# Two gated expert layers: the last two tiles of results placed by TensorE instead of scattered, results weighted by slot, rows numbered by partition

## The reference, cut to what matters

```python
probs = softmax(x @ router_w.T)
w, sel = top_k(probs, 2)
w = w / sum(w)
for g, u, d, c in experts:                     # c: this expert's weight for each token, 0 for most
    h = silu(x @ g) * (x @ u)
    acc = acc + c[:, None] * (h @ d)
x = x + tanh(g_ffn) * acc
```

## Time and profile before

| what | value |
|---|---|
| median of 3 runs | 814.03 us (810.46 to 814.49) |
| the profiled execution | 812.11 us, span of the trace 810.3 us |
| PE busy | 657.9 us, 81% of the span |
| POOL busy | 235.0 us, 29% |
| experts of layer 2, first gather to last result | 471.5 to 543.6 us |
| results of layer 2 kept to statistics done | 543.6 to 558.4 us |
| experts of layer 3, first gather to last scatter issued | 738.3 to 798.2 us |
| from there to the end | 798.2 to 810.3 us |

### The profile page before, as it was taken

One profiled execution on the slowest core, in us unless ns is written; L12 is line 12 of the kernel. 1 busy time (PEld: TensorE's weight loads), 2 busy tenths in 40 slices (PEclk: granted clock), 3 DMA queues, 4 the chain that ended last, 5 costly groups with the idle time before them and its releaser, 6 DMA issues. The chain is left out here.

```text
span 810.3 us, 15372 instructions
## 1 busy us (share of the span) xinstructions
PE 657.9 (81%) x5366; PEld 555.2 (69%) x5366; DVE 406.5 (50%) x1087; ACT 316.5 (39%) x872; POOL 235.0 (29%) x278
## 2 busy tenths in 40 slices
PE   3978789687979999996799889970886999888871
PEld 2647677366869999996568879970543677677761
DVE  4664448674545434432685634434664444254433
ACT  1286123585014444541185035530540344412530
POOL 2033001033144445323100136741700111013773
PEclk9999999998989999998798889995787899988996
DMA  7990000000210000101390001111000000000123
GB/s 228 340 363 1 0 1 1 1 2 1 67 43 18 24 25 23 23 11 65 157 328 1 28 23 48 49 35 53 1 1 1 2 3 2 2 27 23 53 51 103
DMA packets 29006, 45.07 MB, mean 56 GB/s; under 512 B 5458, under 2 KB 18402, under 8 KB 28674
## 3 DMA queue, kind: packets, MB, share of 16 engines
q1 hardware_dynamic: 24514, 35.02, 13.0%
q0 software_dynamic: 4416, 9.05, 4.2%
HBM read 37.44 MB, written 6.62 MB: 54 GB/s over the span
## 5 line engine op out<-in xcount | busy, mean ns | idle before, releaser
L1013 PE MATMUL experts_ps<-experts_act,experts_own 128*128 128x128 f32 x736 | 86.9, 277 | 0.0
L1013 PEld LDWEIGHTS experts_ps<-experts_act,experts_own 128*128 128x128 f32 x736 | 84.9, 194 | 0.1
L1060 ACT ACTIVATE experts_act<-experts_ps,experts_b 128x128 f32<-128x128 f32 x184 | 52.5, 368 | 74.0 <-PE experts_ps L1013 53.7
L1170 PE MATMUL gated_ps_in<-gated_slots_t,gated_own 128*128 128x128 f32 x552 | 70.7, 278 | 2.1 <-DVE gated_slots_t L1231 2.0
L1170 PEld LDWEIGHTS gated_ps_in<-gated_slots_t,gated_own 128*128 128x128 f32 x552 | 65.2, 192 | 4.1 <-DVE gated_slots_t L1231 3.4
L943 POOL DMA_INDIRECT gated_slots<-ffn_tokens,keep_ffn_token x46 | 44.4, 966 | 62.2 <-issue 45.1
L588 POOL TENSOR_TENSOR attention_e<-attention_e,core_inverse 128x1024 f32<-128x1024 f32 x16 | 30.4, 1901 | 100.9 <-DVE core_inverse L705 100.9
L1090 DVE COPY experts_own<-experts_w 128x2048 f32 x23 | 28.2, 1226 | 58.8 <-PE experts_ps L1013 58.8
L943 POOL DMA_INDIRECT experts_slots<-ffn_tokens,keep_ffn_token x23 | 36.6, 1590 | 65.3 <-PE experts_ps L994 45.1
L934 POOL DMA_INDIRECT ffn_results<-gated_results,keep_ffn_row x46 | 45.3, 984 | 20.6 <-DVE gated_results L1242 13.6
L1205 ACT ACTIVATE gated_own<-experts_w_in 128x1024 f32 (+1 forms) x46 | 38.7, 843 | 30.7 <-PEq L776 24.1
(11 more groups left out here) (405 smaller groups left out, 1431.9 us busy)
## 6 DMA issues: line engine op xcount, KB each, us to landing
experts_w<-in_L_ffn_W SPq DMA_DIRECT2D x1, 8192.0 KB, 40.6
experts_w_in<-in_gated_in SPq DMA_DIRECT2D x1, 4096.0 KB, 12.1
combine_mine<-ffn_results SPq DMA_DIRECT2D x12, 256.0 KB, 3.5
experts_w<-in_L_ffn_W SPq DMA_DIRECT2D x1, 2048.0 KB, 12.3
experts_w_out<-in_gated_out SPq DMA_DIRECT2D x1, 2048.0 KB, 16.7
ffn_tokens<-route_xn SPq DMA_DIRECT2D x3, 512.0 KB, 3.2
experts_w_in<-in_L_ffn_gate_w SPq DMA_DIRECT2D x1, 1024.0 KB, 18.9
experts_w_in<-in_L_ffn_up_w SPq DMA_DIRECT2D x1, 1024.0 KB, 21.5
```

The costliest lines, as they stand in the source:

```text
L1013: mm = pe.matmul(ps_2[u][:, c * P:(c + 1) * P], own2[:, u, k, c * P:(c + 1) * P], act1[:, u, k, :], start=(k == 0), stop=(k == chunks - 1))
L1060: act.activation(to[:, u, c, :], source[u][:, c * P:(c + 1) * P], ACT.Gelu, bias=bias[:, bass.ds(e * chunks + c, 1)]).then_inc(done, 1)
L1170: mm = pe.matmul(ps_in[:, j % 2, c * P:(c + 1) * P], own[:, j % 2, c, :], slots_t[:, j % 2, :], start=True, stop=True)
```

## The change

- **Late tiles.** In layers 2 and 3 the results of tiles 21 and 22 (`LATE = 2`) aren't scattered. For each, DVE makes eight 0/1 matrices from slots to tokens (`onehot`) at the start of the stage, and TensorE multiplies them with the tile's results, 16 matmuls of 128x128 in all after the last `down`, summing by token in PSUM. DVE adds the two PSUM banks to x. Since the rows that these slots would fill are loaded all the same, POOL fills a tile with zeros and scatters it to them, twice, after the fourth gather.
- **Weights by slot.** A token's row in the table gets two more numbers (its second weight and the difference of the two), so that rows are 130 numbers, 520 bytes. A small transfer in `route` writes them (1024 pieces of 8 bytes). `keep_result` multiplies by the slot's weight instead of copying, and combining needs plain additions, which run over two tiles at a time: 12 of 128x256 instead of 16 of 128x128.
- **Rows by partition.** A token's row is 8p + t instead of 128t + p, in all three layers, so that a partition's results lie side by side; a load reads 2 KB in a piece instead of two pieces of 1 KB.
- **Loads.** In layers 2 and 3 two are issued by SP and two by ACT.
- A gather waits for `weighed` (the slot's weight was read, on DVE) as well as for `turned`.

The core of the diff:

```diff
-        self.tokens = nc.dram_tensor(f"{name}_tokens", [T, D], F32, kind="Internal").ap()
+        self.tokens = nc.dram_tensor(f"{name}_tokens", [T, D + 2 if late else D], F32, kind="Internal").ap()
...
+                if routes.late:
+                    sp.wait_ge(sem["weights_ready"], 2)
+                    sp.dma_start(routes.tokens[:, D:D + 2].rearrange("(p t) d -> p t d", p=P), routes.slot_weight[:])\
+                        .then_inc(sem["tokens_stored"], 16)
+                sp.wait_ge(sem["tokens_stored"], 32 if routes.late else 16)
...
+        if j == AHEAD - 1 and routes.late:
+            pool.memset(zeros[:], 0.0).then_inc(sem["zeroed"], 1)
+            pool.wait_ge(sem["zeroed"], 1)
+            for late in range(TILES - routes.late, TILES):
+                pool.indirect_dma_start(routes.results, bass.IndirectOffsetOnAxis(ap=routes.row_of[:, late:late + 1], axis=0),
+                                        zeros[:], None).then_inc(keep.zeros_scattered, 16)
-    for j in range(TILES - lag, TILES):
+    for j in range(TILES - lag, TILES - routes.late):
         scatter(j)
...
+                def place(n):
+                    j = late_tiles[n]
+                    pe.wait_ge(sem["onehot_made"], n + 1)
+                    pe.wait_ge(sem["result_kept"], j + 1)
...
+                    for t in range(NT):
+                        mm = pe.matmul(combine.late[t // 4][:, (t % 4) * D:(t % 4 + 1) * D], onehot[:, n, t, :],
+                                       results[:, j % AHEAD, :], start=(n == 0), stop=(n == LATE - 1),
+                                       skip_group_check=True)
...
-                    dve.tensor_copy(results[:, j % AHEAD, :], ps_y[:, j % 2, 0:D]).then_inc(sem["result_kept"], 1)
+                    dve.tensor_scalar(results[:, j % AHEAD, :], ps_y[:, j % 2, 0:D], slot_gain[:, j % AHEAD:j % AHEAD + 1],
+                                      None, ALU.mult).then_inc(sem["result_kept"], 1)
...
-        rows = self.routes.results[FIRST_ROW:SPARE, :].rearrange("(t p k) d -> p t (k d)", k=CHOSEN, p=P)
+        rows = self.routes.results[FIRST_ROW:SPARE, :].rearrange("(p t k) d -> p t (k d)", k=CHOSEN, p=P)
...
-                    block.sync(combine.load)
+                    block.sync(lambda sp: combine.load(sp, (0, 1)))
+                    block.scalar(lambda act: combine.load(act, (2, 3)))
```

More of the change, by code:

```diff
@@ L865, in _ @@
                         "p (k t) -> p k t", k=CHOSEN), gate, -1.0, ALU.mult, ALU.mult))
+                if routes.late:
+                    steps.wait(dve)
+                    dve.tensor_copy(routes.slot_weight[:, :, 0], routes.weight[:, 1, :]).then_inc(sem["weights_ready"], 1)
+                    dve.tensor_tensor(routes.slot_weight[:, :, 1], routes.weight[:, 0, :], routes.weight[:, 1, :],
+                                      ALU.subtract).then_inc(sem["weights_ready"], 1)
                 dve.wait_ge(sem["counted"], 1)
@@ L924, in expert_index, with move_tiles @@
     return engine.value_load(routes.expert_of[0:1, bass.ds(j, 1)], min_val=0, max_val=EXPERTS - 1)
-def move_tiles(pool, keep, sem, routes, slots, results, lag, beside=None):
+def move_tiles(pool, keep, sem, routes, slots, results, lag, beside=None, zeros=None):
     def scatter(j):
@@ L1231, in keep_slots @@
                     dve.tensor_copy(slots_t[:, j % 2, :], ps_x[:, 0:P]).then_inc(sem["slots_kept"], 1)
+                    u = j % AHEAD
+                    if j >= AHEAD:
+                        dve.wait_ge(sem["result_kept"], j - AHEAD + 1)
+                    dve.scalar_tensor_tensor(out=slot_gain[:, u:u + 1], in0=slots[:, u, D + 1:D + 2],
+                                             scalar=second[:, j:j + 1], in1=slots[:, u, D:D + 1], op0=ALU.mult,
+                                             op1=ALU.add).then_inc(sem["weighed"], 1)
                 def multiply(j):
@@ L1289, in stats, with add_weighted, weighted_stats @@
             rows.stats_of_tile(dve, t)
+        def add_weighted(dve):
+            for k in range(CHOSEN):
+                for b in range(B):
+                    if k == 0:
+                        dve.wait_ge(self.loaded[b], 16)
+                    else:
+                        dve.wait_ge(self.added, b + 1)
+                    dve.tensor_tensor(x[:, 2 * b:2 * b + 2, :], x[:, 2 * b:2 * b + 2, :],
+                                      self.mine[:, 2 * b:2 * b + 2, k, :], ALU.add).then_inc(self.added, 1)
+            for n in range(B):
+                dve.wait_ge(self.late_made, 1 + n // 2)
+                dve.wait_ge(self.added, B + n + 1)
+                dve.tensor_tensor(x[:, 2 * n:2 * n + 2, :], x[:, 2 * n:2 * n + 2, :],
+                                  self.late[n // 2][:, (n % 2) * 2 * D:(n % 2 + 1) * 2 * D].rearrange("p (t d) -> p t d", d=D),
+                                  ALU.add).then_inc(self.done, 1)
+                if rows and n:
+                    weighted_stats(dve, n - 1)
+            if rows:
+                weighted_stats(dve, B - 1)
+                rows.join_stats(dve)
+        def weighted_stats(dve, n):
+            dve.wait_ge(self.done, n + 1)
+            for t in (2 * n, 2 * n + 1):
+                rows.stats_of_tile(dve, t)
         @block.vector
         def _(dve):
+            if self.routes.late:
+                add_weighted(dve)
+                return
             for t in range(NT):
```

93 lines of the change are left out of this document (71 added, 22 removed).

## The result

The changed kernel takes 805.29 us (median of 20 runs, 799.12 to 812.21), the kernel before 810.59 (20 runs, 805.5 to 814.97). The ratio is 0.9919, 95% interval [0.9903, 0.9935]: 6.6 us of 810.6 less, between 5.3 and 7.9 (it leaves out the one disturbed execution of the changed kernel, 812.21 us, which is the profiled one).

The account below looks back on a forecast made before the run. It took TensorE to set layer 2's pace and POOL's indirect transfers layer 3's. Terms -3.5 + 0 + 0.3 gave -3.2 us: 808.9 from the profiled execution, 810.8 from the median, middle 809.9 forecast; range 805.5 to 814.

Parts of the forecast that it names:

- The rest of the block is as before.: Layer 2, behind the last statistics: nothing changes up to the next attention, which stays 6.49 us behind the power.
- my sum: Whole kernel: layer 2 -3.5, layer 3 0, work added elsewhere +0.3, together -3.2 us.
- With the same 2.38 us between, the loads start at 542.0.: Layer 2's end: loads wait for tile 20's scatter, started at 539.63, and start at 542.0 instead of 546.2.
- Landing 4.7: Layers 2 and 3: all loads land 4.7 us behind the first issue, the middle between 4.0 and 5.4.
- Additions and statistics: Layer 2's end: adds 0.37 us each, seven after the last landing 2.6; four late adds and eight statistics 3.1.
- placing: Layer 2's end: sixteen matmuls on TensorE take about 4.6 us, to 547.9, ahead of the late adds at 549.3.
- The tail: Layer 2, last result kept to last statistics: 8.8 us instead of 12.30, a gain of 3.5, between 2.3 and 4.7.
- Layer 3: Layer 3's experts and combining: last scatter 0.9 us earlier, adds ending almost unchanged; gain 0, between 1.8 gained and 1.4 lost.
- Gathers of 520 bytes: Rival, gathers on POOL: longer rows could stretch each gather; at 1.833 us, 16.5 lost in layer 3, 822 to 824; chance 0.10.
- The two steps in the routing: `route`, DVE's chain: two small steps and a wait cost 0.1 to 0.5 us per layer, 0.3 for both.
- The 0/1 matrices: Start of the experts: making `onehot` takes DVE about 3.7 us, covered by 6.68 us in which it had idled.
- The fast rival: Layers 2 and 3: loads and adds both at their best, -6.3 us, 805.8 to 807.7; chance 0.15.

Follow-up runs that it names:

- e1: The kernel before with only a POOL drain added right behind the last scatter of each gated stage: ratio 0.9963 to the kernel before, 3.0 us less.
- e2: The changed kernel with only the POOL drain behind its last scatter taken out: ratio 0.9969 to the kernel before, 2.5 us less.
- e8: The changed kernel with ten unused matmuls more in the routing of layers 1 and 2: ratio 0.9929 to the kernel before.
- e4: The changed kernel with all four loads issued by SP: ratio 0.9931 to the kernel before.

## Why the prediction was wrong

- **"The rest of the block is as before."** This step failed. I took the end of the block to be the power (its end, 558.4, stands in the table of stages), and saw the drain behind it neither in the trace of before nor in the diff. The time from power to attention stood in the trace: 6.5 us, in nearly all of which no engine was busy. It gave 3.74 us, more than any term of my sum; e1 and e2 show it from both sides. Without it the change brings 2.5 us (e2), near the 3.2 of the sum.
- **"With the same 2.38 us between, the loads start at 542.0."** The mechanism was right, the size off: 4.29 and 3.67 instead of 2.38, since the last scatter fell together with a fetch of TensorE's program (shown by e8). In the kernel before, that scatter wasn't the last, and nothing waited for it; its landing stood in the trace, 2.98 behind its start, where the last one's, from which I took the 2.38, was 2.24. One data packet of the scatter's 16 was late, and the landing with it, by 1.4 and 2.0 us (in the changed kernel it started at 542.35, the other fifteen by 540.83); why that one alone, the trace doesn't show.
- **Landing 4.7.** It was 5.44 and 5.07 in layer 2, 5.74 and 5.68 in layer 3: around the upper bound of 5.4 and above it. I had no row for the middle. The second queue didn't shorten it: with all four loads on one queue (e4) it took 5.21 and 5.18.
- **Additions and statistics.** The additions followed each other at 0.34 for 0.37 ((2.44 - 0.42) / 6), late additions and statistics 2.96 for 3.1, placing 3.74 for 4.6, and TensorE was done 4.6 us ahead of the late additions. The tail gave 1.6 and 2.4 instead of 3.5: 1.9 and 1.3 lost on the scatter, 0.7 and 0.4 on the landing, 0.6 to 0.8 won back as less was left for DVE when the last load came.
- **Layer 3.** The fifth gather 2.6 later for 2.7, the last scatter 0.98 earlier for 0.9, additions ending 0.8 later behind it, as the sum had it. That last number is luck: the loads landed 1.0 later than I had it, and 3.1 of additions stood behind the last one instead of 4.1. With the four stores due at once the end came 0.8 later behind the additions instead of 0.2: a loss of 0.5 to 0.6 in all where I had 0, between 1.8 gained and 1.4 lost. The 1.8 doesn't come out of its own terms, which give 1.3 at the additions' end and 0.8 at the last store.
- **The rest.** Gathers of 520 bytes took 0.967 us in the median, as before: that rival is out. (My price for it was wrong too: at 1.833 the sum gives 825 to 827, not 822 to 824, which count the gain twice.) The two steps in the routing cost 0.24 in layer 2 (13.95 from the first search for an expert, `FIND_INDEX8`, to the first gather, 13.71 before) and nothing in layer 3 (14.00, 14.13 before), where DVE had waited 0.27 for TensorE. The 0/1 matrices took 3.66 for 3.7, covered. The fast rival came close in its number (-6.3) by luck and not in its mechanism: the loads did not land faster.

## What to carry to other kernels

A block's end is work: look at the stretch between the last busy engine and the first of the next block, list what the sequencers do there, and read a diff for lines that are no operation. A drain on GpSimd behind indirect transfers cost time wherever it stood here (1.7 to 3.85 us), so put it where others are busy. When a change makes another transfer the last one, take the landing of that one from the trace, not that of its neighbours.

## What the runs showed of the hardware

- POOL's drain costs more the more indirect transfers were issued since the last one (2.25 us with 23, 3.49 with 42, 3.82 with 46), even long after they have landed: in the kernel before, 3.84 us though the last one had been issued 12.8 us earlier and landed 2.24 us behind its issue.
- TensorE's program arrives in packets of 16 KB, six of them in the 72 us of layer 2's experts, and data wait for them: in the changed kernel one data packet of tile 20's scatter started only as such a packet ended (542.35 against 542.36, the other fifteen by 540.83). A scatter that lands in 2.25 us otherwise (median) took 2.8 to 4.3 where one began 0.6 to 2.0 us behind its start.
